# Maxima of two heads in the two row halves of the array, operands loaded in a new row order

## The chip, the cores and the metric

The kernel runs on one core of a Trainium2 chip. The metric is the device time of one execution in microseconds; three runs of the kernel before gave 3184.15, 3186.4 and 3193.72 us.

## What is computed

The reference takes `x` of shape (8, 1024, 256) through four stages, each `x = x + layernorm(stage(layernorm(x)))`: a causal softmax attention with low-rank projections, a feed-forward stage, a causal attention with quadratic features, and a last feed-forward stage with ternary weights. The change touches the two attentions:

```python
# first attention, per batch, 16 heads of width 16
scores = jnp.einsum('bqhd,bkhd->bhqk', Q, K) / math.sqrt(D_K)
scores = jnp.where(causal, scores, -jnp.inf)
attn = jax.nn.softmax(scores, axis=-1)
out = jnp.einsum('bhqk,bkhd->bqhd', attn, V)
...
# second attention: a running sum of features, computed by the kernel as squared scores
num = jnp.einsum('bhtf,bhtfd->bhtd', phi_q, kv_cum)
den = jnp.einsum('bhtf,bhtf->bht', phi_q, jnp.cumsum(phi_k, axis=2))[..., None] + EPS
```

## The kernel before

The program runs nine passes one after the other. Those that matter here: `latent_pass` and `features_pass` compute queries, keys and values of all heads and store them in DRAM; `attend_pass` loads them, once with `softmax=True` (its tiles carry `a_` in the profile) and once with `softmax=False` (`b_`).

**Operands.** Queries and keys are held as three bf16 parts (high, middle, low) whose sum is the f32 value. A product of two such numbers is taken as six products of parts, and these lie under one another as contraction rows: `Q_STACK` and `K_STACK` say which part goes into which group of 16 rows, six groups, 96 rows (`STACK`). In the softmax pass two further rows (96 and 97) hold the negated maximum of each query, split in two, against ones in the keys, so that a score comes out with its maximum already taken off (98 rows).

**Units and rings.** A unit is four heads of one batch with all 1024 positions; there are 32 (`UNITS`). Operands sit in a ring of three buffers (`qs`, `ks`, `vs`). `all_units` runs a loop of ten turns with three units each, and two units behind it.

**SP.** `load(n, r)` issues 13 transfers for a unit: six for the queries, six for the keys, each of 16 rows with 8 KB a row into 16 partitions, and one of 512 KB for the values. The load of unit n+2 is issued when all weighings of unit n-1 are done. `load_rows(n+1)` issues eight small transfers that place the peak rows in `qs`, when VectorE has made them; `store` writes a unit's sums.

**TensorE.** A unit has 12 steps (`STEPS`). Steps 0 to 3 belong to the first half of the queries, with 512, 384, 256 and 128 columns, steps 4 to 11 to the second half, with 512 columns in steps 4 to 8 and 384, 256, 128 in the last three. In step s TensorE computes the scores of step s+2 (`scores`, L896, two heads at a time, two matmuls each) and weighs the values with the exponentials of step s (`weigh`, L910, f32, each head in its own 32 columns of the array). Steps 10 and 11 thus compute the first scores of unit n+1, and `operands` waits there, at step 10, for its load and its peak rows.

**Maxima.** The maximum of each query is found ahead: `maximum_scores` (L886) computes a chunk of up to 512 score columns (queries as the weights of the array) into one of three PSUM banks, VectorE reduces it (`maxima`, L844 a plain maximum, L846 with the causal mask added) and frees the bank. There are 36 chunks per unit, nine per head. Each step has three slots for a chunk: behind the first two scores, behind the second two, and behind the weighing. Slots 0 to 17 of unit n carry the second half of the chunks of unit n+1, slots 18 to 35 the first half of those of unit n+2; at slot 18 TensorE waits for the load of unit n+2 (L930). When the chunks of unit n+1 are done, VectorE closes them (`largest`, L852 to L860) and SP issues the row loads (L735).

**ScalarE and GpSimd.** ScalarE takes the exponentials of two heads at a time from PSUM (L793, squares in the second attention, where VectorE does the fourth head, L820 and L823), GpSimd masks the diagonal blocks (L772).

TensorE and the others take their work strictly in the order in which it is written. The lines that set the places:

```python
                for c in range(a, b):
                    hd, pieces = chunks[c]
                    pe.wait_ge(s_taken, CH * n + c + 1)
...
                    half = CH // 2
                    if k < half and ahead:
                        maximum_scores(n + 1, (r + 1) % RING, half + k, half + k + 1)
                    if k >= half and far:
                        if k == half:
                            pe.wait_ge(loaded[(r + 2) % RING], LOADED * (rnd + (r + 2) // RING) + LOADED)
```

Of the kernel before, what the change touches and what calls it, by code (L numbers as in the profile page):

```python
# [29 lines left out]
F32 = mybir.dt.float32  # L30
# [11 lines left out]
Q_STACK = ((0, 0, 3), (1, 0, 2), (2, 0, 1))  # L42
K_STACK = ((0, 1, 3), (0, 1, 2), (0, 1, 1))
STACK = 16 * 6

# [41 lines left out]
class Resident:  # L87


    def __init__(self, nc, ctx, z):  # L90
# [33 lines left out]
        self.v_dram = nc.dram_tensor("values", [z.UNITS, z.S, P], F32, kind="Internal").ap()  # L124
# [315 lines left out]
def latent_pass(nc, z, m):  # L440
    G, DC, GROUPS = z.G, z.DC, z.TILES // z.G
    with ExitStack() as ctx:
# [18 lines left out]
        def _(sp):  # L461
# [3 lines left out]
            def store(i, u):  # L465
                n = 2 * i + u
                sp.wait_ge(vx_ready, 2 * n + 3)
                for t in range(G):
                    at = u * z.GT + t * P
                    sp.dma_start(m.v_dram[bass.ts(i, z.UPB), at:at + P, :].rearrange("g p k -> p g k"),  # L470
                                 vx[u][:, t, :, :].rearrange("p (g h) k -> p g (h k)", g=z.UPB)).then_inc(stored[u], 16)
# [151 lines left out]
def store_parts(eng, z, m, parts, stored, i, u):  # L623

    for part in range(PARTS):
        for j in range(4):
            eng.dma_start(m.qk_dram[part, j // 2, bass.ds(i * z.D + (j % 2) * P, P), u * z.GT:(u + 1) * z.GT],
                          parts[:, part, j, :]).then_inc(stored, 16)
# [4 lines left out]
def attend_pass(nc, z, m, softmax):  # L633
# [20 lines left out]
    chunks = [(hd, pieces) for hd in range(HPU) for pieces in (  # L654
# [3 lines left out]
    CH = len(chunks)  # L658
    assert CH == 3 * STEPS
    SRING = 3  # L660
    with ExitStack() as ctx:
# [13 lines left out]
        LOADED = 16 * (2 * STACK // z.DK + 1)  # L675
# [4 lines left out]
        if softmax:  # L680
# [8 lines left out]
             rows_ready, ones_ready) = sm("bias_zero", "bias_ready", "peak_set", "s_ready", "s_taken", "npeak_ready",  # L689
                                          "high_ready", "split_ready", "rows_ready", "ones_ready")  # L690
            ROWS_LOADED = 16 * 8
        else:
            twin = sb("twin", [P, 512], F32, 2)
            twin_ready, d_ready = sm("twin_ready", "d_ready")
        block = ctx.enter_context(nc.Block())

# [17 lines left out]
        def _(sp):  # L714
# [1026 lines left out]
```

## Time and profile before

| | us |
|---|---|
| median of three runs | 3186.4 |
| the profiled execution | 3190.47 |
| its span on the core | 3188.3 |
| TensorE busy | 2571.1 (81%) |
| VectorE busy | 2393.3 (75%) |
| ScalarE busy | 1702.3 (53%) |
| GpSimd busy | 918.0 (29%) |
| closing reductions of the softmax pass, first and last start | 301.8 and 1284.6 |
| first score matmul of the second attention | 2282.04 |

A busy share says little by itself: TensorE's work in a matmul pass overlaps, and an average over the span mixes stages. What counts in a stage is the order of events in one unit, which the timeline gives, and who waited for whom. The chain that ended last accounts for the end of the program only (a few per cent of the span), so the two attention passes have to be read from their own stretches.

### The profile page before, as it was taken

The numbers are of one execution on the slowest core, as the hardware profiler recorded it, in microseconds if no ns is written. First come the engines' busy times: TensorE is split into PE (matmuls) and PEld (weight loads), VectorE is DVE, ScalarE is ACT, GpSimd is POOL, SyncE is SP. The second block draws the span as 40 slices with busy tenths as digits, with TensorE's granted clock in tenths as the row PEclk, the third lists the DMA queues.
The fourth block names the chain that finished last, engine by engine and source line by source line (L and its number), as shares of the span: only waits on it lengthen the run. The fifth ranks groups of instructions, "written<-read, shape, count | busy, mean of one in ns | idle before, by whom it ended". The sixth has DMA issues, their size and how long they took to land. (4 is left out here: it accounts for less than half of the span.)

```text
span 3188.3 us, 60438 instructions
## 1 busy us (share of the span) xinstructions
PE 2571.1 (81%) x15239; PEld 1172.0 (37%) x15239; DVE 2393.3 (75%) x5816; ACT 1702.3 (53%) x2778; POOL 918.0 (29%) x844
## 2 busy tenths in 40 slices
PE   2885998988898989576889886878499999995536
PEld 1441332333333333254555554545122222223425
DVE  5886777877787777257999996999476666665975
ACT  0441666655666555443333333766277777773544
POOL 0340111111111111173444442222222222223834
PEclk9895999989999999888999998999699999997879
DMA  5687445454545454240000000455788888863302
GB/s 160 185 270 143 80 74 93 77 89 75 92 79 88 77 90 70 73 165 1 0 0 0 0 0 14 127 163 159 155 141 137 143 135 141 139 119 112 122 10 95
DMA packets 285075, 310.22 MB, mean 97 GB/s; under 512 B 39504, under 2 KB 239136, under 8 KB 272672
## 3 DMA queue, kind: packets, MB, share of 16 engines
q1 hardware_dynamic: 284960, 309.07, 46.4%
q14 instruction: 90, 0.74, 0.1%
q8 instruction: 25, 0.41, 0.1%
HBM read 181.55 MB, written 126.88 MB: 97 GB/s over the span
## 5 line engine op out<-in xcount | busy, mean ns | idle before, releaser
L793 ACT ACTIVATE a_p<-psum 128x1024 f32<-128x1024 f32 (+3 forms) x768 | 590.0, 813 | 385.6 <-PE psum L896 385.3
L846 DVE CUSTOM_DVE_ANT_0 a_dump<-psum,a_bias 128x256 bf16<-128x256 f32 (+3 forms) x1024 | 451.9, 487 | 180.3 <-PE psum L886 154.2
L886 PE MATMUL psum<-a_ks,a_qs 96*128 96x512 bf16 (+3 forms) x1536 | 467.7, 350 | 133.9 <-DMA a_vs<-values 112.7
L793 ACT ACTIVATE b_p<-psum 128x512 f32<-128x512 f32 (+5 forms) x768 | 453.4, 653 | 168.1 <-PE psum L896 167.3
L772 POOL TENSOR_SCALAR_AFFINE_SELECT a_p<-a_p 128x512 f32<-128x512 f32 x256 | 162.9, 636 | 888.5 <-ACT a_p L793 888.5
L896 PE MATMUL psum<-a_qs,a_ks 98*128 98x512 bf16 (+3 forms) x1536 | 395.7, 341 | 5.4 <-ACT a_p L793 3.7
L844 DVE TENSOR_REDUCE a_peak<-psum 128x1 f32<-128x512 f32 x512 | 333.2, 686 | 35.4 <-PE psum L886 34.6
L896 PE MATMUL psum<-b_qs,b_ks 96*128 96x512 bf16 (+3 forms) x1536 | 320.8, 331 | 39.2 <-DMA b_vs<-values 38.9
L910 PE MATMUL psum<-a_p,a_vs 128*32 128x512 f32 (+3 forms) x3072 | 348.3, 527 | 0.6 <-POOL a_p L772 0.4
L820 DVE COPY b_twin<-psum 128x512 f32<-128x512 f32 (+3 forms) x384 | 213.3, 555 | 175.8 <-PE psum L896 174.1
L910 PE MATMUL psum<-b_p,b_vs 128*32 128x512 f32 (+3 forms) x3072 | 328.8, 500 | 8.0 <-POOL b_p L772 8.0
L886 PEld LDWEIGHTS psum<-a_ks,a_qs 96*128 96x128 bf16 x1536 | 135.9, 99 | 497.3 <-issue 163.8
L772 POOL TENSOR_SCALAR_AFFINE_SELECT b_p<-b_p 128x512 f32<-128x512 f32 x256 | 162.8, 636 | 469.6 <-DVE b_p L823 440.2
L1359 PE MATMUL psum<-f_xt,w_fc 128*128 128x512 f32 x512 | 247.8, 646 | 56.6 <-ACT f_xt L1298 50.8
L1121 PE MATMUL psum<-wo,m_att 128*128 128x256 f32 x512 | 146.7, 452 | 125.5 <-POOL m_att L1068 95.9
L823 DVE SCALAR_TENSOR_TENSOR b_p<-psum,b_twin 128x512 f32<-128x512 f32 (+3 forms) x384 | 214.4, 558 | 40.3 <-PE psum L910 0.5
L896 PEld LDWEIGHTS psum<-b_qs,b_ks 96*128 96x128 bf16 x1536 | 109.9, 98 | 343.8 <-issue 174.2
L1269 POOL TENSOR_TENSOR f_parts<-f_rest,f_parts 128x512 bf16<-128x512 f32 x128 | 179.5, 1402 | 167.4 <-DVE f_parts L1228 167.4
L896 PEld LDWEIGHTS psum<-a_qs,a_ks 98*128 98x128 bf16 x1536 | 150.3, 101 | 118.8 <-ACT a_p L793 34.4
L1225 DVE TENSOR_TENSOR f_rest<-f_hid,f_parts 128x512 f32<-128x512 f32 x128 | 191.1, 1493 | 1.6 <-ACT f_parts L1312 1.6
L1370 PE MATMUL psum<-w_proj,f_parts 128*128 128x256 bf16 x1536 | 172.2, 274 | 6.4 <-POOL f_parts L1269 6.4
L1359 PEld LDWEIGHTS psum<-f_xt,w_fc 128*128 128x128 f32 x512 | 105.1, 208 | 191.0 <-issue 183.0
(186 smaller groups left out, 3496.5 us busy)
## 6 DMA issues: line engine op xcount, KB each, us to landing
qk_parts<-l_parts SPq DMA_DIRECT2D x192, 128.0 KB, 1.7
a_qs<-qk_parts SPq DMA_DIRECT2D x192, 128.0 KB, 4.6
a_ks<-qk_parts SPq DMA_DIRECT2D x192, 128.0 KB, 7.6
qk_parts<-g_parts SPq DMA_DIRECT2D x192, 128.0 KB, 1.7
b_qs<-qk_parts SPq DMA_DIRECT2D x192, 128.0 KB, 4.5
b_ks<-qk_parts SPq DMA_DIRECT2D x192, 128.0 KB, 7.6
values<-l_vx SPq DMA_DIRECT2D x64, 256.0 KB, 2.9
a_vs<-values SPq DMA_DIRECT2D x32, 512.0 KB, 10.1
```

The costliest lines, as they stand in the source:

```text
L772: pool.affine_select(out=diag, in_=diag, compare_op=ALU.is_ge, fill=0.0, base=0, pattern=[[0, HPU], [1, P]], channel_multiplier=-1).then_i ...
L793: act.activation(p[s % SLOTS][:, 2 * k:2 * k + heads, q0(s):512], m.psum[:, at:at + heads, q0(s):512], ACT.Exp if softmax else ACT.Square, ...
L820: dve.tensor_copy(twin[s % 2][:, q0(s):512], bank).then_inc(twin_ready, 1)
L823: dve.scalar_tensor_tensor(out=p[s % SLOTS][:, 3, q0(s):512], in0=bank, scalar=1.0 / z.DK, in1=twin[s % 2][:, q0(s):512], op0=ALU.mult, op ...
L844: last = dve.tensor_reduce(dst, piece, AX.X, ALU.max)
L846: last = dve.tensor_tensor_reduce(dump[c % SRING][:, at:at + w], piece, bias[:, 512 - w:], 1.0, NEG, ALU.add, ALU.max, dst)
L886: last = pe.matmul(m.bank[SB + c % SRING][:, at:at + w], qs[r][0:STACK, hd, qt * P:(qt + 1) * P], ks[r][0:STACK, hd, h * 512:h * 512 + w], ...
L896: last = pe.matmul(m.bank[score_bank(s, hd)][:, q0(s):512], ks[r][0:ROWS, hd, kt * P:(kt + 1) * P], qs[r][0:ROWS, hd, h * 512 + q0(s):(h + ...
L910: last = pe.matmul(m.bank[OB[h]][32 * hd:32 * hd + 32, q0(s):512], vs[r][:, kt, 32 * hd:32 * hd + 32], p[s % SLOTS][:, hd, q0(s):512], sta ...
L1225: dve.tensor_tensor(rest[c % 4][:, :], hid[c % 4][:, :], parts[u][:, 0, c, :], ALU.subtract).then_inc(rest_ready, 1)
L1269: pool.tensor_tensor(parts[u][:, 2, j, :], rest[j % 4][:, :], parts[u][:, 1, j, :], ALU.subtract).then_inc(low_ready, 1)
L1359: last = pe.matmul(m.bank[F0 + j % 4], m.w_fc[:, c, j * P:(j + 1) * P], xt[u][:, c, :], start=(c == 0), stop=(c == DC - 1))
```

## The change

The six products of parts get new places, and different ones for heads 0, 1 and heads 2, 3 of a unit. For heads 0 and 1 the four largest products fill rows 0 to 63 and the other two rows 64 to 95. For heads 2 and 3 the three largest fill rows 64 to 111 and the other three rows 0 to 47; rows 48 to 63 are zero. The maxima now use only rows 0 to 63 of a head 0 or 1 and rows 64 to 111 of a head 2 or 3, so the two matmuls of a pair of heads lie in different row halves of the array. A chunk becomes a pair of chunks, 18 per unit, put into the odd slots only; one wait covers both. `EARLY = 6` of the 18 pairs are computed two units ahead, the other 12 one unit ahead, so the last pair of unit n+1 stands in slot 23 of unit n, and the wait for the load of unit n+2 in slot 25.

The peak rows move to rows 112 and 113 (`TOP`). Scores use 114 rows; in the second attention 96 for heads 0 and 1, 112 for heads 2 and 3. Rows that no load fills are filled once per pass by VectorE: 12 fills before its first other work, and TensorE waits for all of them, SP's first load of each buffer for its own.

A load is now 14 transfers of queries and keys with 4 KB a row, ten of them into 32 partitions (two products at a time, their rows interleaved, which is the same in queries and keys) and four into 16, and one for the values, whose DRAM layout changes so that a partition's 4 KB lie together. The order of the parts in DRAM changes to fit (`Q_SLOT`, `K_SLOT`).

```diff
-Q_STACK = ((0, 0, 3), (1, 0, 2), (2, 0, 1))
-K_STACK = ((0, 1, 3), (0, 1, 2), (0, 1, 1))
+Q_SLOT = (1, 2, 0)
+K_SLOT = (1, 0, 2)
 STACK = 16 * 6
+MAIN = 16 * 4
+TOP = 16 * 7
...
-        self.v_dram = nc.dram_tensor("values", [z.UNITS, z.S, P], F32, kind="Internal").ap()
+        self.v_dram = nc.dram_tensor("values", [z.UNITS, P, z.ST, P], F32, kind="Internal").ap()
...
             def load(n, r):
-                for tile, which, stack in ((qs[r], 0, Q_STACK), (ks[r], 1, K_STACK)):
-                    row = 0
-                    for first, step, groups in stack:
-                        for part in range(groups):
-                            src = m.qk_dram[first + step * part, which, bass.ts(n, HPU * z.DK), :]
-                            sp.dma_start(tile[row:row + z.DK, :, :].rearrange("p h t -> p (h t)"),
-                                         src.rearrange("(d h) t -> d (h t)", h=HPU)).then_inc(loaded[r], 16)
-                            row += z.DK
...
+                half = z.S * HPU // 2
+                for par, runs in enumerate((((0, 1, 2, 0, 2), (32, 2, 2, 0, 2), (64, 0, 0, 1, 2)),
+                                            ((64, 1, 2, 0, 2), (96, 2, 1, 1, 1), (0, 2, 1, 0, 1), (16, 0, 0, 1, 2)))):
+                    heads = slice(par * half, (par + 1) * half)
+                    for row, q_slot, q_wide, k_slot, groups in runs:
+                        into = slice(row, row + z.DK * groups)
...
+            for r in range(RING):
+                for tile, fill in ((qs[r], 0.0), (ks[r], 1.0)):
+                    dve.memset(tile[32:MAIN, HPU // 2:HPU, :], 0.0)
+                    last = dve.memset(tile[STACK:P, 0:(HPU if softmax else HPU // 2), :], fill)
+                last.then_inc(rows_set, 1)
...
+                for j in range(a, b):
+                    pe.wait_ge(s_taken, CH * n + 2 * j + 2)
+                    for piece, (qt, h, at, w) in enumerate(chunks[j][1]):
+                        for par in range(2):
+                            hd, half = chunks[j][0] + par * HPU // 2, (slice(0, MAIN), slice(MAIN, TOP))[par]
...
+                    if not softmax or k % 2 == 0:
                         return
...
+                    j = k // 2
+                    if j < CP - EARLY and ahead:
+                        maximum_scores(n + 1, (r + 1) % RING, EARLY + j, EARLY + j + 1)
+                    if j >= CP - EARLY and far:
+                        if j == CP - EARLY:
                             pe.wait_ge(loaded[(r + 2) % RING], LOADED * (rnd + (r + 2) // RING) + LOADED)
```

What stands in a row on TensorE, in the softmax pass, from a weighing in step 4 to the wait for the load in step 6 of a unit (`a_ks1`, `a_qs1`: the buffers of unit n+1; an ISA row is a wait), before:

```order
L910 MATMUL psum<-a_p0,a_vs0 32x512 x4
...
L910 MATMUL psum<-a_p1,a_vs0 32x512 x4
L884 REGISTER_ALU
L886 MATMUL psum<-a_ks1,a_qs1 128x512
L892 REGISTER_ALU
L896 MATMUL psum<-a_qs0,a_ks0 128x512 x2
L930 ISA
L884 ISA
L886 MATMUL psum<-a_ks2,a_qs2 128x128
L886 MATMUL psum<-a_ks2,a_qs2 128x384
```

And now, with a unit in buffer 1, from the weighing of step 6 to the same wait, which stands in step 8:

```order
L937 MATMUL psum<-a_p2,a_vs1 32x512 x4
...
L937 MATMUL psum<-a_p3,a_vs1 32x512 x4
L906 REGISTER_ALU
L910 MATMUL psum<-a_ks2,a_qs2 128x512 x2
L918 REGISTER_ALU
L923 MATMUL psum<-a_qs1,a_ks1 128x256 x2
L918 REGISTER_ALU
L923 MATMUL psum<-a_qs1,a_ks1 128x256 x2
L957 ISA
L906 ISA
L910 MATMUL psum<-a_ks0,a_qs0 128x128 x2
```

The last maxima of the next unit, behind a weighing, and the wait that follows them moved two steps down, toward step 10; each maximum is now two matmuls.

On TensorE in two full steps of the same pass, steps 4 and 5 of a unit, from the first scores of step 5 on, with the new order:

```order
L923 MATMUL psum<-a_qs1,a_ks1 128x512 x2
L906 REGISTER_ALU
L910 MATMUL psum<-a_ks2,a_qs2 128x128 x2
L910 MATMUL psum<-a_ks2,a_qs2 128x384 x2
L918 REGISTER_ALU
L923 MATMUL psum<-a_qs1,a_ks1 128x512 x2
L937 MATMUL psum<-a_p1,a_vs1 32x512 x4
L906 REGISTER_ALU
L910 MATMUL psum<-a_ks2,a_qs2 128x512 x2
```

Before, each of these steps had a maximum behind each of the three groups; now an odd step has a pair in its first and third place and an even step one in its second.

On VectorE at the start of the softmax pass (`a_qs0`, `a_ks0`: buffer 0), before and now:

```order
L830 MEMSET a_ks0 2x4096
L830 MEMSET a_ks1 2x4096
L830 MEMSET a_ks2 2x4096
L832 MEMSET a_peak0 128x64
L846 ISA a_dump0,a_peak0<-psum,a_bias0 128x128
```

```order
L836 MEMSET a_qs0 32x1024
L837 MEMSET a_qs0 32x2048
L836 MEMSET a_ks0 32x1024
L837 MEMSET a_ks0 32x4096
L836 MEMSET a_qs1 32x1024
L837 MEMSET a_qs1 32x2048
```

Three fills became twelve (the rows shown repeat for buffers 1 and 2). In the second attention, where there were none, the same twelve stand with 1024, 1024, 1024 and 2048 elements.

## Rows read from the trace of the kernel before

**Rows 1.** Table of stretches: stretch and length, busy us (count) per engine, clock, DMA.
```profile
core 0: us, PE busy (x) PEld busy (x) DVE busy (x) ACT busy (x) POOL busy (x), PEclk, DMA share, GB/s
500.00:900.00 400.00, 356.45 (x2433) 127.09 (x2433) 311.42 (x1062) 241.55 (x329) 64.80 (x102) 0.94 0.51 84
...
2500.00:2900.00 400.00, 384.59 (x2980) 109.44 (x2978) 273.62 (x497) 307.75 (x537) 104.29 (x164) 0.99 0.77 128
```

**Rows 2.** One line's instructions: the closing reduction of a unit's maxima.
```profile
L852 DVE TENSOR_REDUCE a_npeak<-a_peak x32: 219/220/221, 301.8 to 1284.6; 128x32 f32<-128x64 f32 x32
```

**Rows 3.** TensorE's waits, 330 to 1310 us: total us, times, longest.
```profile
PE psum L886 <- DMA a_vs<-values: 79.8, 26, 4.1
PE psum L886 <- DVE a_peak L846: 17.8, 9, 2.1
```

**Rows 4.** Timeline of TensorE, 664 to 732 us: start, us, instruction.
```profile
667.07 0.60 PE L896 MATMUL psum<-a_qs,a_ks 98*128 98x512 bf16 x2
...
671.25 0.60 PE L896 MATMUL psum<-a_qs,a_ks 98*128 98x512 bf16 x2
...
709.69 0.60 PE L896 MATMUL psum<-a_qs,a_ks 98*128 98x512 bf16 x2
...
710.78 0.38 PE L886 MATMUL psum<-a_ks,a_qs 96*128 96x128 bf16 x2
711.09 1.06 PE L910 MATMUL psum<-a_p,a_vs 128*32 128x512 f32 x8
712.09 0.39 PE L886 MATMUL psum<-a_ks,a_qs 96*128 96x512 bf16 x1
712.31 0.60 PE L896 MATMUL psum<-a_qs,a_ks 98*128 98x512 bf16 x2
...
714.71 0.39 PE L886 MATMUL psum<-a_ks,a_qs 96*128 96x512 bf16 x1
...
719.83 0.39 PE L886 MATMUL psum<-a_ks,a_qs 96*128 96x512 bf16 x1
...
724.02 0.60 PE L896 MATMUL psum<-a_qs,a_ks 98*128 98x512 bf16 x2
...
731.96 0.38 PE L896 MATMUL psum<-a_qs,a_ks 98*128 98x512 bf16 x1
```

**Rows 5.** VectorE's waits, 330 to 1310 us, the one in its own issue.
```profile
DVE a_dump L846 <- issue: 23.4, 10, 2.7
```

**Rows 6.** Timeline of VectorE and of SP's queue, from the closing reduction on.
```profile
716.02 0.22 DVE L852 TENSOR_REDUCE a_npeak<-a_peak 128x32 f32<-128x64 f32 x1
...
717.07 4.96 SPq L735 DMA_DIRECT2D a_qs<-a_rows  x8
```

**Rows 7.** DMA issues: tiles, count, KB each, median us to landing.
```profile
a_qs<-a_rows SPq DMA_DIRECT2D x256, 2.0 KB, 1.8
```

**Rows 8.** Timeline of all engines, 676 to 684 us: a maximum and its reduction.
```profile
676.27 0.39 PE L886 MATMUL psum<-a_ks,a_qs 96*128 96x512 bf16 x1
...
676.85 0.69 DVE L846 CUSTOM_DVE_ANT_0 a_dump<-psum,a_bias 128x512 bf16<-128x512 f32 x1 [0.67 <-PE psum L886]
```

**Rows 9.** Timeline of VectorE in the first unit's maxima, the same chunk two heads apart.
```profile
281.54 0.28 DVE L846 CUSTOM_DVE_ANT_0 a_dump<-psum,a_bias 128x128 bf16<-128x128 f32 x1
...
292.89 0.28 DVE L846 CUSTOM_DVE_ANT_0 a_dump<-psum,a_bias 128x128 bf16<-128x128 f32 x1
```

**Rows 10.** Timeline of all engines at the start of the softmax pass.
```profile
262.76 3.47 DVE L830 MEMSET a_ks<- 2x4096 bf16 x1 [14.62 <-PEq L72]
...
267.03 3.47 DVE L830 MEMSET a_ks<- 2x4096 bf16 x1 [0.80 <-issue]
...
278.05 1.44 PE L886 MATMUL psum<-a_ks,a_qs 96*128 96x128 bf16 x5 [32.87 <-DMA a_vs<-values]
```

**Rows 11.** Timelines of SP's queue and of TensorE at the start of the second attention.
```profile
2265.29 2.67 SPq L724 DMA_DIRECT2D b_qs<-qk_parts  x6
...
2282.04 3.17 PE L896 MATMUL psum<-b_qs,b_ks 96*128 96x512 bf16 x8 [38.90 <-DMA b_vs<-values]
```

More of the change, by code:

```diff
@@ L650, in attend_pass @@
     SLOTS = 4
-    chunks = [(hd, pieces) for hd in range(HPU) for pieces in (
+    chunks = [(hd, pieces) for hd in range(HPU // 2) for pieces in (
         ((0, 0, 0, 128), (2, 0, 128, 384)), ((3, 0, 0, 512),), ((1, 0, 0, 256), (5, 1, 256, 256)),
@@ L657, in attend_pass @@
         ((7, 0, 0, 512),), ((7, 1, 0, 512),))]
-    CH = len(chunks)
+    CP = len(chunks)
+    CH = 2 * CP
     assert CH == 3 * STEPS
     SRING = 3
+    EARLY = 6
     with ExitStack() as ctx:
@@ L674, in attend_pass @@
         st_ready, p_ready, masked, pv_done, o_taken = sm("st_ready", "p_ready", "masked", "pv_done", "o_taken")
[L675 removed]
+        LOADED = 16 * 15
         STORED = 16
@@ L694, in attend_pass, with operand_rows @@
             twin_ready, d_ready = sm("twin_ready", "d_ready")
+        rows_set, = sm("rows_set")
         block = ctx.enter_context(nc.Block())
+        def operand_rows(hd):
+            if softmax:
+                return slice(0, TOP + 2)
+            return slice(0, STACK) if hd < HPU // 2 else slice(0, TOP)
         def q0(s):
@@ L828, in _ @@
                 return
-            for r in range(RING):
-                last = dve.memset(ks[r][STACK:STACK + 2, :, :], 1.0)
-            last.then_inc(ones_ready, 1)
             dve.memset(peak[:, :, :], NEG).then_inc(peak_set, 1)
@@ L837, in maxima @@
             def maxima(n, a, b):
-                for c in range(a, b):
-                    hd, pieces = chunks[c]
+                for c in range(2 * a, 2 * b):
+                    hd, pieces = chunks[c // 2][0] + c % 2 * HPU // 2, chunks[c // 2][1]
                     wait_alone(dve, s_ready, CH * n + c + 1, m.alone)
@@ L877, in _ @@
             pe.sem_inc(pv_done, PV)
-            if softmax:
-                pe.wait_ge(ones_ready, 1)
+            pe.wait_ge(rows_set, RING)
             def maximum_scores(n, r, a, b):
-                for c in range(a, b):
-                    hd, pieces = chunks[c]
-                    pe.wait_ge(s_taken, CH * n + c + 1)
-                    for qt, h, at, w in pieces:
-                        last = pe.matmul(m.bank[SB + c % SRING][:, at:at + w], qs[r][0:STACK, hd, qt * P:(qt + 1) * P],
-                                         ks[r][0:STACK, hd, h * 512:h * 512 + w], start=True, stop=True)
-                    last.then_inc(s_ready, 1)
+                for j in range(a, b):
[3 more added lines that the diff above has]
+                            hd, half = chunks[j][0] + par * HPU // 2, (slice(0, MAIN), slice(MAIN, TOP))[par]
+                            last = pe.matmul(m.bank[SB + (2 * j + par) % SRING][:, at:at + w],
+                                             qs[r][half, hd, qt * P:(qt + 1) * P],
+                                             ks[r][half, hd, h * 512:h * 512 + w], start=True, stop=True)
+                            if piece == len(chunks[j][1]) - 1:
+                                last.then_inc(s_ready, 1)
             def scores(n, r, s, k):
@@ L921, in some_maxima @@
                 def some_maxima(k):
-                    if not softmax:
+                    if not softmax or k % 2 == 0:
                         return
-                    half = CH // 2
-                    if k < half and ahead:
-                        maximum_scores(n + 1, (r + 1) % RING, half + k, half + k + 1)
-                    if k >= half and far:
-                        if k == half:
+                    j = k // 2
[3 more added lines that the diff above has]
+                        if j == CP - EARLY:
                             pe.wait_ge(loaded[(r + 2) % RING], LOADED * (rnd + (r + 2) // RING) + LOADED)
-                        maximum_scores(n + 2, (r + 2) % RING, k - half, k - half + 1)
+                        maximum_scores(n + 2, (r + 2) % RING, j - CP + EARLY, j - CP + EARLY + 1)
                 for s in range(STEPS):
```

47 lines of the change are left out of this document (30 added, 17 removed).

## Prediction, made before the changed kernel ran

> **What bounds the kernel now.** I read the table of stretches first [rows 1]. In the softmax attention pass TensorE is busy 356.45 of 400 us at a granted clock of 0.94, VectorE 311.42, ScalarE 241.55; in the second attention pass TensorE has 384.59 of 400 us at 0.99. So both passes are TensorE's, and only the first has time between its instructions. The first pass is a chain of 32 units: the reduction that closes a unit's maxima starts 32 times between 301.8 and 1284.6 us [rows 2], 982.8 / 31 = **31.70 us per unit**.
>
> What fills a unit is read from TensorE's timeline where the clock is high and nothing waits [rows 4]: steps 4 to 11, 0 and 1 run from 709.69 to 731.96 (22.27 us), steps 2 and 3 from 667.07 to 671.25 (4.18 us), together 26.45 us. The waits [rows 3] are 79.8 / 31 = 2.57 us per unit for the loads of the unit after next (met at slot 18 of 36) and 17.8 / 31 = 0.57 us for VectorE. The last follows stalls of up to 2.7 us in VectorE's own issue, ten of them, one per turn of the loop [rows 5]. 31.70 - 26.45 - 3.14 leaves 2.1 us, the price of the stretches at the lower clock: 6% off the mean clock of a 31.7 us unit is 1.9.
>
> **The gain: maxima in pairs.** A full step [rows 4] takes 2.62 us (709.69 to 712.31) and has three maxima of 512 columns at 0.22 (712.09 to 712.31). Run two heads at a time, 18432 columns of a unit become 9216: at 0.22 per 512 that takes 18 x 0.22 = 4.0 us off a unit. No row here shows two row halves at work together; the nearest is the weighing, whose eight f32 pieces in four column strips take 1.00 us (711.09 to 712.09). I take full overlap, and keep none at all for a rival.
>
> **The gain: the load.** The wait of 2.57 us goes, whatever the new transfers take: slot 18 becomes slot 25, two steps (over 4 us) later, and the longest wait was 4.1 us [rows 3]. Transfers that land sooner are then worth nothing more.
>
> **What takes the place of that wait.** Before, the maxima of unit n+1 end at slot 17 of unit n; with EARLY = 6 they end at slot 23, and the scores of unit n+1 still begin at step 10. Between lies a chain: last maximum, VectorE, four small VectorE operations, eight loads of peak rows from SP, TensorE. Before [rows 4, 6, 7]: slot 17 at 714.71, the closing reduction at 716.02, the first row load at 717.07, eight issues of 4.96 us to 722.03, and the last, issued about 0.6 us before that, lands 1.8 us after its issue, at 723.2. Step 10 starts at 724.02, so 0.8 us was to spare.
>
> After, from the start T of the pair in slot 23: 0.58 us to VectorE (676.27 to 676.85 [rows 4, 8]), two reductions of 0.63 and 0.69, a gap of 0.1, so the closing reduction starts at T+2.0; then 1.05 + 4.96 + 1.2 as before: rows there at **T+9.2**. TensorE gets to step 10 sooner. VectorE finishes the pair at T+1.9, the small operations at T+3.0, the first chunk of the pair of slot 25 at T+3.7, of slot 27 at T+5.0; the pair of slot 29 needs that, and step 10 is reached at T+5.3. TensorE then stands still 3.9 us in each unit, SP, VectorE and ScalarE behind it. The load that SP issues for the next unit isn't moved by it.
>
> **The rest of the cycle**, from step 10 to the pair of slot 23 of the next unit, is ten steps with 15 pairs. Before it took 22.26 us [rows 4]: 724.02 to 731.96, plus 4.18, plus 709.69 to 719.83. VectorE takes 18 chunks from 281.54 to 292.89 [rows 9], 0.63 each, 1.26 per pair. But a pair may only start when one chunk is left to VectorE (three banks), and from the end of a reduction to the start of the next, through TensorE, 0.67 us pass [rows 8]; with 0.63 of cover and the start of a waiting instruction I take 1.35 per pair, 1.26 at least. In two full steps TensorE has twice a pair, a weighing and one head pair's scores (0.22 + 1.09 + 0.43 = 1.74), and once a pair and both scores (0.22 + 0.87 = 1.09, VectorE's 1.35 counts): 4.83, so the four full steps 9.7 against 10.1 before. The six narrow steps have nine pairs, VectorE's: 12.1, what they take now. Together 21.8 us; with 1.26 throughout 9.5 + 11.3 = 20.8.
>
> A warm unit is then 9.2 + 21.8 = 31.0 us. VectorE's issue stall stays, 0.6. The wait of 3.9 us is as long as the one that goes, so the clock falls after it as now; half of the work behind it is VectorE's, which doesn't feel the clock, so I take 1.4 instead of 2.1. **33.0 us per unit, 1.3 more than now, 31 x 1.3 = +40 us.** The low end is 9.2 + 20.8 with 0.3 for all else, 30.3 (-43 us).
>
> **Switching between shapes.** A weighing starts 0.31 us after the maximum ahead of it (710.78 to 711.09), where one of the same shape follows after 0.22, and its 1.00 us (to 712.09) is 0.12 over the 0.88 of four streams of 512 columns at 0.22. Entering and leaving another shape thus shows 0.21 us, beside full-array instructions. A pair between scores enters and leaves too. My sum puts this at nothing, since part of the 0.21 may be the f32 weight loads'; with it in full, a pair holds TensorE 0.43: two full steps 1.95 + 1.95 + 1.35 = 5.25, the four 10.5, the narrow ones 12.7 where TensorE and VectorE hold each other up, a unit 9.2 + 23.2 + 0.6 + 1.8 = 34.8.
> The Trainium skill, page "TensorEngine Tiling (Array Packing)", section "Key Properties", says that a change of tiling mode drains the engine, while tiles of one mode run in parallel; by its first half the unit is the 34.8 us just given, by its "Theoretical Speedup" alone 33.0. The 0.31 against 0.22 speaks for a drain; nothing in this trace shows one for row halves.
>
> **Starts of the two passes.** The new fills count, by the program, 8192 elements per buffer in the first pass (zeros are filled two to an element). Fills of 4096 start 4.27 us apart (262.76 to 267.03 [rows 10]): three buffers 25.6 us, to 288.4, and TensorE waits for all; it began at 278.05: **+10** (+6 by their 3.47 us of busy time). The first load waits 8.5 us for its buffer's fills and then takes its 16 us at most, to 288, so no more. The first unit's maxima are VectorE's in both versions and the shorter second set there only uncovers the row chain: 0, within 3 either way. In the second pass 5120 elements per buffer are 16.0 us, against the 16.75 us that TensorE waits anyway (2265.29 to 2282.04 [rows 11]); the load starts 5.3 us later and may be faster: 0 to +5, taken as **+2**. Its steady part stays, since TensorE is full and 112 rows stream like 96. The stores of values keep their number and size, with rows that lie further apart: 0 (up to +5).
>
> **Sum**: 40 + 10 + 2 = +52 us. The profiled execution took 3190.47 us with a span of 3188.3 and lies 4.1 us above the median of 3186.4; I set the sum on the median: **3238 us**. A measurement of this kernel tells about 0.3%, 10 us, from no change.
>
> **Rivals.**
> *Faster (0.20)*: the pass is freed as meant. VectorE isn't held up between pairs and the clock, with TensorE less loaded but never far behind, hardly falls: 30.3 us per unit, -43 + 12 = -31, 3155 us. For it: VectorE needs only 36 x 0.63 + 1.05 = 23.7 us per unit, ScalarE 19. Against: the row chain of 9.2 us starts a third of a unit later than now. It decides at 31.0 us per unit, below that the kernel is faster.
> *The drain (0.22)*: 34.8 us per unit, +96 + 12 = +108, 3294 us. For it the 0.31 against 0.22, against it that no row shows the halves.
> *The halves don't overlap (0.05)*: a pair costs 0.44 and the switches 0.21: two full steps 2.17 + 2.17 + 1.52, the four 11.7, the narrow ones 12.1 + 9 x 0.21 = 14.0, 37.3 per unit, +174 + 12 = +186, 3372 us. The change then doesn't do what it says.
> *No change (0.10)*: the two effects cancel at 31.3 us per unit, 3186 us with the longer start.
> *The forecast (0.43)*: 32 to 34 us per unit, 3207 to 3270 us, taken at 33.0.
>
> **Range and chances.** From 3160, which leaves out the better half of the faster case, to 3320, which leaves out the serial case and the worst of the drain. Slower by over 0.3%: 0.43 + 0.22 + 0.05 = 0.70; within: 0.10; faster: 0.20.
>
> **What would show it.** The closing reductions of the first pass stand 33 us apart; the waits of TensorE show one for the peak rows about 31 times, near 4 us, and none for the values; the loads land well ahead; matmuls of the two halves start together or 0.22 us apart, and the first score matmul behind a pair comes after 0.22 or more like 0.43; VectorE's waits for maxima shorten but don't vanish; TensorE begins the first pass near 288 us and the second near 2280 to 2287, shifted by what came before. I am wrong if the rows are there before step 10, which needs the chain in under 5.5 us, or if the four full steps between end up far under 9.5 us.

## The result, and the profile after

The changed kernel took **3293.8 us** (median of four runs, 3290.6 to 3297.7), the kernel before, run beside it, 3190.1 us: a ratio of 1.0315, with an interval of 1.0295 to 1.0335. It is slower by 103.8 us. Forecast were +52 us, 3238, with a range of 3160 to 3320.

From the page of the changed kernel, the two groups of TensorE's matmuls in the softmax pass, scores (L923) and maxima (L910), with busy us, mean ns, and the idle time ahead of them:

```profile
L923 PE MATMUL psum<-a_qs,a_ks 114*128 114x512 bf16 (+3 forms) x1536 | 394.0, 363 | 122.6 <-DMA a_qs<-a_rows 119.3
...
L910 PE MATMUL psum<-a_ks,a_qs 64*128 64x512 bf16 (+7 forms) x1536 | 243.0, 356 | 146.0 <-DVE a_peak L870 64.6
```

The table of stretches, with the columns of [rows 1], in the softmax pass and in the second attention:

```profile
500.00:900.00 400.00, 327.39 (x2268) 83.43 (x2266) 296.70 (x980) 229.53 (x308) 59.22 (x94) 0.90 0.27 80
...
2600.00:3000.00 400.00, 383.75 (x2972) 109.36 (x2968) 272.49 (x496) 306.83 (x536) 104.02 (x164) 0.99 0.43 128
```

The second attention is what it was, TensorE full, with half the DMA share. In the softmax pass every engine does less per microsecond than before: TensorE 327 of 400 us where it had 356, VectorE 297 where it had 311 [rows 1]. Nothing became the bound by being full. The closing reductions, which answer to [rows 2], tell the length of a unit:

```profile
L876 DVE TENSOR_REDUCE a_npeak<-a_peak x32: 219/220/222, 318.0 to 1378.4; 128x32 f32<-128x64 f32 x32
```

1060.4 / 31 = **34.2 us per unit** against 31.70. That alone is 77.6 us. The whole of the span's +104.3 us (3292.6 against 3188.3) divides at these two reductions and at the first score matmul of the second attention (2381.88 now, 2282.04 before [rows 11]):

| stretch | before | after | difference |
|---|---|---|---|
| start to the first closing reduction | 301.8 | 318.0 | +16.2 |
| 31 units | 982.8 | 1060.4 | +77.6 |
| last closing reduction to the second attention's first score | 997.4 | 1003.5 | +6.1 |
| from there to the end | 906.3 | 910.7 | +4.4 |

TensorE's waits in the softmax pass, 350 to 1380 us (total, times, longest), beside [rows 3]:

```profile
PE psum L923 <- DMA a_qs<-a_rows: 112.8, 30, 3.9
PE psum L910 <- DVE a_peak L870: 50.0, 71, 1.2
PE psum L910 <- DVE a_peak L868: 26.1, 38, 2.1
```

The wait for the values is gone. In its place is one for the peak rows, in every unit, 112.8 / 30 = 3.76 us each. The chain behind it, from the timeline of all engines (start, us, instruction; SPq is the issue of SP's queue), from the pair in slot 23 to the scores of step 10:

```profile
728.58 0.39 PE L910 MATMUL psum<-a_ks,a_qs 64*128 64x512 bf16 x2
...
730.50 0.22 DVE L876 TENSOR_REDUCE a_npeak<-a_peak 128x32 f32<-128x64 f32 x1
...
731.86 5.00 SPq L757 DMA_DIRECT2D a_qs<-a_rows  x8
...
738.13 1.89 PE L923 MATMUL psum<-a_qs,a_ks 114*128 114x512 bf16 x4 [3.70 <-DMA a_qs<-a_rows]
```

From 728.58 to 738.13 are 9.55 us. The last row shows a second thing: four score matmuls take 1.89 us there, and 1.05 where TensorE has been busy for a while (718.99 below). The granted clock is 0.50 from 738.2 to 740.0 us, which is half speed, the 1.2 GHz level, and it comes right behind the wait.

Finally the pairs, from TensorE's timeline: a row that bounds the full steps, then a pair between scores, a pair behind a weighing and one ahead of a weighing:

```profile
718.99 1.05 PE L923 MATMUL psum<-a_qs,a_ks 114*128 114x512 bf16 x4
...
721.40 0.60 PE L923 MATMUL psum<-a_qs,a_ks 114*128 114x512 bf16 x2
721.93 0.39 PE L910 MATMUL psum<-a_ks,a_qs 64*128 64x128 bf16 x4
722.26 0.60 PE L923 MATMUL psum<-a_qs,a_ks 114*128 114x512 bf16 x2
...
723.79 0.39 PE L910 MATMUL psum<-a_ks,a_qs 64*128 64x512 bf16 x2
724.11 1.04 PE L923 MATMUL psum<-a_qs,a_ks 114*128 114x512 bf16 x4
725.08 0.39 PE L910 MATMUL psum<-a_ks,a_qs 64*128 64x512 bf16 x2
725.40 1.06 PE L937 MATMUL psum<-a_p,a_vs 128*32 128x512 f32 x8
```

Two matmuls of 512 columns together last 0.39 us, as one did before (714.71 in [rows 4]): the two halves do work at the same time. But the next instruction comes 0.32 us after the pair (725.08 to 725.40), and the pair itself starts late: four score matmuls at 0.22 would end 0.86 us after 724.11, the pair starts after 0.97. Between scores, 0.86 us pass from the two score matmuls at 721.40 to those at 722.26; the scores alone take 0.43 of it, so the pair holds TensorE 0.43 us, and two single maxima held it 0.44.

### The profile page after: what moved, and what is told of

It is laid out like the page before. It is cut to its first block and busy times, and to the rows that moved or that the text cites. A ratio compares the mean times of both kernels' runs of the same rounds, so it can differ in the third digit from the quotient of the medians.

```text
span 3292.6 us, 60468 instructions
## 1 busy us (share of the span) xinstructions
PE 2543.1 (77%) x15239; PEld 1082.0 (33%) x15239; DVE 2436.9 (74%) x5837; ACT 1706.1 (52%) x2778; POOL 917.0 (28%) x844
## 5 line engine op out<-in xcount | busy, mean ns | idle before, releaser
L870 DVE CUSTOM_DVE_ANT_0 a_dump<-psum,a_bias 128x128 bf16<-128x128 f32 (+3 forms) x1024 | 445.2, 488 | 75.9 <-PE psum L910 70.0
L923 PE MATMUL psum<-a_qs,a_ks 114*128 114x512 bf16 (+3 forms) x1536 | 394.0, 363 | 122.6 <-DMA a_qs<-a_rows 119.3
L910 PE MATMUL psum<-a_ks,a_qs 64*128 64x512 bf16 (+7 forms) x1536 | 243.0, 356 | 146.0 <-DVE a_peak L870 64.6
L923 PE MATMUL psum<-b_qs,b_ks 96*128 96x512 bf16 (+7 forms) x1536 | 320.9, 330 | 41.4 <-DMA b_vs<-values 40.8
L1386 PE MATMUL psum<-f_xt,w_fc 128*128 128x512 f32 x512 | 250.1, 651 | 58.1 <-ACT f_xt L1325 52.2
L923 PEld LDWEIGHTS psum<-a_qs,a_ks 114*128 114x128 bf16 x1536 | 105.0, 101 | 413.2 <-issue 211.8
L923 PEld LDWEIGHTS psum<-b_qs,b_ks 96*128 96x128 bf16 (+1 forms) x1536 | 110.2, 98 | 345.0 <-issue 214.6
L910 PEld LDWEIGHTS psum<-a_ks,a_qs 64*128 64x128 bf16 (+1 forms) x1536 | 59.8, 95 | 414.1 <-DVE a_peak L870 190.9
L1148 PEld LDWEIGHTS psum<-wo,m_att 128*128 128x128 f32 x512 | 116.9, 234 | 163.2 <-issue 108.6
```

Source lines behind the costliest of these rows:

```text
L870: last = dve.tensor_tensor_reduce(dump[c % SRING][:, at:at + w], piece, bias[:, 512 - w:], 1.0, NEG, ALU.add, ALU.max, dst)
L910: last = pe.matmul(m.bank[SB + (2 * j + par) % SRING][:, at:at + w], qs[r][half, hd, qt * P:(qt + 1) * P], ks[r][half, hd, h * 512:h * 512 ...
L923: last = pe.matmul(m.bank[score_bank(s, hd)][:, q0(s):512], ks[r][live, hd, kt * P:(kt + 1) * P], qs[r][live, hd, h * 512 + q0(s):(h + 1) ...
L1148: last = pe.matmul(bank, att[u][:, c, t * P:(t + 1) * P], wo[:, c, :], start=(c == 0), stop=(c == DC - 1))
L1386: last = pe.matmul(m.bank[F0 + j % 4], m.w_fc[:, c, j * P:(j + 1) * P], xt[u][:, c, :], start=(c == 0), stop=(c == DC - 1))
```

## The experiments

Each kernel was measured against the kernel before on the same chip (its median was 3192.8 us in the first set, 3196.0 in the second). "A" is my theory throughout: the place of the last maxima, ahead of a chain of 9 us, sets the unit, and the clock behind the wait adds to it.

### Nine pairs early in place of six

The changed kernel with one number changed, so that the last pair of unit n+1 stands in slot 17, where its last chunk stood before.

```diff
-    EARLY = 6
+    EARLY = 9
```

> The changed kernel with EARLY = 9: nine pairs two units ahead and nine one unit ahead, so that the last pair of the next unit stands in slot 17 again, as before the change, and the wait for the load in slot 19. Theory A (the chain from the last maximum to the peak rows sets the unit, 34.2 us): TensorE's wait of 3.8 us for the peak rows is gone and with it most of the lower clock; the closing reductions stand about 29.5 us apart, the kernel takes some 3150 us. Theory B (the switches between array shapes and the round trip between TensorE and VectorE cost it, the wait only fills time that would be lost anyway): the reductions stay 33 us apart or more, 3255 us or more. The loads, now in 12 us after the unit's start, are there at slot 19 in both.

Measured: **3125.0 us**, ratio 0.9797 (0.9772 to 0.9822). A unit takes (1210.7 - 317.5) / 31 = 28.8 us. The closing reduction, TensorE's waits from 350 to 1180 us, and that stretch in the table (clock 0.99, third value from the end):

```profile
L876 DVE TENSOR_REDUCE a_npeak<-a_peak x32: 219/220/222, 317.5 to 1210.7; 128x32 f32<-128x64 f32 x32
```
```profile
PE psum L910 <- DVE a_peak L870: 58.1, 90, 2.5
...
PE psum L910 <- DMA a_vs<-values: 15.3, 15, 1.6
```
```profile
350.00:1180.00 830.00, 747.17 (x5564) 201.35 (x5560) 718.02 (x2436) 554.53 (x754) 147.52 (x232) 0.99 0.30 92
```

The wait for the rows is gone and the clock is back with it, as theory A had it; the unit came out shorter than its 29.5 us. Of the change, the 12 pairs that stood one unit ahead instead of nine cost 169 us: 5.4 us per unit. Over this stretch TensorE's idle time per unit is 3.6 us less than in the changed kernel (82.8 us in 28.8 units against 157.8 in 24.3), and its busy time, for the same matmuls, 1.8 us less (25.9 against 27.7 us per unit), which goes with the clock (0.99 against 0.90). One place shows the clock's part by itself, steps 10 and 11 of a unit, at full clock here and behind the wait in the changed kernel:

```profile
706.61 1.04 PE L923 MATMUL psum<-a_qs,a_ks 114*128 114x512 bf16 x4
...
710.51 0.61 PE L923 MATMUL psum<-a_qs,a_ks 114*128 114x256 bf16 x4
```

They take 3.90 us, against 6.07 for the same instructions there (704.67 to 710.74, shown further below).

### The late place alone, in the kernel before

The kernel before with 24 chunks one unit ahead and 12 two units ahead, in place of 18 and 18: the same shift, without pairs, new loads or fills.

```diff
-                    half = CH // 2
-                    if k < half and ahead:
-                        maximum_scores(n + 1, (r + 1) % RING, half + k, half + k + 1)
+                    early = CH // 3
+                    late = CH - early
+                    if k < late and ahead:
+                        maximum_scores(n + 1, (r + 1) % RING, early + k, early + k + 1)
```

> The kernel before with the place of the maxima alone changed: 24 of the 36 single chunks one unit ahead, 12 two units ahead, so that the last chunk of the next unit stands in slot 23 and the wait for the load in slot 24. Theory A: the wait for the loads (2.57 us a unit) goes and one for the peak rows of about 4.4 us comes (the chain of 8.5 us against 4.2 us for steps 8 and 9); the unit goes from 31.7 to 33.5 or 34, the kernel to about 3250 us. Theory B (only pairs make the place harmful): the unit falls to 28 or 29 us, the kernel to about 3090 us.

Measured: **3299.3 us**, ratio 1.033 (1.0306 to 1.0355), 35.0 us per unit. The closing reduction and the wait for the rows, 350 to 1180 us:

```profile
L852 DVE TENSOR_REDUCE a_npeak<-a_peak x32: 219/220/223, 301.6 to 1387.7; 128x32 f32<-128x64 f32 x32
```
```profile
PE psum L896 <- DMA a_qs<-a_rows: 74.4, 23, 3.6
```

The place alone makes the kernel before as slow as the whole change does: +3.3 us per unit. The wait it makes is 3.2 us per unit (74.4 / 23), and the wait for the values that it takes away was 2.57 [rows 3]; the granted clock of 350 to 1180 us fell from 0.93 to 0.88. The difference of the two waits, 0.6, is the small part of it. TensorE's idle time in that stretch went from 3.4 to 4.6 us per unit (its waits for VectorE grew too, from 0.7 to 1.35), and its busy time, for the same matmuls, from 28.3 to 30.4: 2.1 of the 3.3 us go with the clock. The expectation for theory A was a wait of 4.4 us and a unit of 33.5 to 34; the wait came out shorter and the unit longer.

### The pairs without the row halves

The changed kernel with both matmuls of a pair over rows 0 to 111, so that they can't overlap.

```diff
-                            hd, half = chunks[j][0] + par * HPU // 2, (slice(0, MAIN), slice(MAIN, TOP))[par]
+                            hd, half = chunks[j][0] + par * HPU // 2, slice(0, TOP)
```

> The changed kernel with its pairs as they are, but each maximum taken over rows 0 to 111 (all six products) instead of one row half, so the two matmuls of a pair follow each other in the full array, without a change of shape and without overlap. The trace of the changed kernel shows a pair of 512 columns at 0.32 us plus 0.11 ahead of it, 0.43 together. Theory A (the change of shape costs what the overlap saves): a pair takes 0.44, the unit stays within 0.3 us of 34.2 and the kernel within 10 us of 3294. Rival (the overlap brings its 4 us a unit and the switches are free): the unit grows by 2 us or more where TensorE is the bound, the kernel by 60 us or more.

Measured: **3316.8 us**, ratio 1.0374 (1.0345 to 1.0403), (1405.9 - 319.0) / 31 = 35.06 us per unit: 0.86 more than the changed kernel, 23 us in all. The granted clock of 350 to 1180 us is 0.94 here and 0.90 there, and the wait for the rows 3.5 us instead of 3.76, so the 0.86 is what remains after both. From its timeline:

```profile
732.33 0.61 PE L910 MATMUL psum<-a_ks,a_qs 112*128 112x512 bf16 x2
732.86 1.07 PE L937 MATMUL psum<-a_p,a_vs 128*32 128x512 f32 x8
733.86 0.60 PE L923 MATMUL psum<-a_qs,a_ks 114*128 114x512 bf16 x2
734.30 0.60 PE L910 MATMUL psum<-a_ks,a_qs 112*128 112x128 bf16 x4
734.74 0.60 PE L923 MATMUL psum<-a_qs,a_ks 114*128 114x512 bf16 x2
...
736.27 0.61 PE L910 MATMUL psum<-a_ks,a_qs 112*128 112x512 bf16 x2
736.71 1.03 PE L923 MATMUL psum<-a_qs,a_ks 114*128 114x512 bf16 x4
```

Two matmuls here last 0.61 against 0.39, so the halves do overlap in the changed kernel. A pair over all rows holds TensorE 0.44 us between scores (734.30 to 734.74), in the halves 0.43: no gain. Ahead of a weighing it is 0.53 (732.33 to 732.86) against 0.43 with the entry, behind one 0.44 (736.27 to 736.71) against 0.32 (723.79 to 724.11). So the overlap is worth 0.1 us where the neighbour on one side is a weighing, which changes shape anyway, and nothing elsewhere; 12 of a unit's 18 pairs have such a neighbour. Neither number expected of this run came out: it lies between the 10 us of A and the 60 of its rival.

### The loads alone

The kernel before with the new loads and nothing else: single maxima in the old places, 98 rows, no fills of zeros. Since each transfer carries all four heads it has 8 KB a row, 256 KB, and a unit takes seven transfers (13 before, 15 in the changed kernel). The values have the changed layout.

```diff
-Q_STACK = ((0, 0, 3), (1, 0, 2), (2, 0, 1))
-K_STACK = ((0, 1, 3), (0, 1, 2), (0, 1, 1))
+Q_SLOT = (1, 2, 0)
+K_SLOT = (1, 0, 2)
...
+                for row, q_slot, q_wide, k_slot in ((0, 1, 2, 0), (32, 2, 2, 0), (64, 0, 0, 1)):
+                    into = slice(row, row + 2 * z.DK)
+                    src = parts[0][:, q_slot:q_slot + (1 if q_wide else 2), :]
+                    if q_wide:
+                        src = src.to_broadcast([z.DK, 2, z.S * HPU])
+                    sp.dma_start(q[into, :], src).then_inc(loaded[r], 16)
+                    sp.dma_start(k[into, :], parts[1][:, k_slot:k_slot + 2, :]).then_inc(loaded[r], 16)
+                sp.dma_start(vs[r][:, :, :], m.v_dram[bass.ts(n, 1), :, :, :].rearrange("n p k c -> p (n k) c")
```

> The kernel before with the loads alone changed: two products at a time into 32 partitions with their rows interleaved (six transfers of 256 KB for queries and keys), the values laid out so that a partition's 4 KB lie together; 96 and 98 rows, single maxima and their slots as before, no new fills. Theory A: the load lands before slot 18, TensorE's wait of 2.57 us a unit goes with part of the lower clock (2.1 us), nothing else moves in; 28 us a unit, 31 x 3.5 = 110 us less, about 3080 us. Rival (the load is not what the wait is for, or the peak rows, with 0.8 us to spare, take its place): a unit of 30.5 us or more, 3150 us or more.

Measured: **3049.0 us**, ratio 0.9548 (0.9527 to 0.957): the fastest of all, 27.4 us per unit. The closing reduction, the only wait of TensorE above 2.1 us in all from 350 to 1180 us, that stretch, and the load of the values with its landing (median us):

```profile
L854 DVE TENSOR_REDUCE a_npeak<-a_peak x32: 219/220/220, 297.4 to 1148.0; 128x32 f32<-128x64 f32 x32
```
```profile
PE psum L888 <- DVE a_peak L848: 17.9, 9, 2.1
```
```profile
350.00:1180.00 830.00, 805.54 (x5813) 289.89 (x5809) 714.72 (x2458) 581.78 (x795) 155.11 (x244) 1.00 0.36 93
```
```profile
a_vs<-values SPq DMA_DIRECT2D x32, 512.0 KB, 6.5
```

TensorE is busy 806 of 830 us at full clock. A unit is 4.26 us shorter than before; the wait for the values, 2.57, and the price of the lower clock, which the prediction had put at 2.1, come to 4.7. The nine-pair version above, whose loads differ from these in rows of 4 KB and 15 transfers, is 76 us slower: 1.4 us per unit, and 20 us more ahead of the first closing reduction (317.5 against 297.4). Per unit its TensorE waits 2.0 us for VectorE (58.1 / 28.8), here 0.6, and 0.5 for the values, here nothing; that last part may be the loads' and not the pairs', and without it 0.9 us per unit remain. **The pairs, with their row order and its fills, are a loss even in the right place.**

### The row loads from two queues

The changed kernel, with four of a unit's eight row loads issued from ScalarE, behind its exponentials of step 11, and four from SP. This shortens the chain and touches nothing else.

```diff
-                for k in range(2):
-                    at = qs[r][TOP + k:TOP + k + 1, :, :].rearrange("o h (q b i) -> o (h q) b i", b=4, i=32)
...
+                place_rows(sp, n, r, 0)
...
+                    if s == STEPS - AHEAD - 1 and softmax and ahead:
+                        place_rows(act, n + 1, (r + 1) % RING, 1)
```

> The changed kernel, its order of pairs unchanged (last pair of the next unit in slot 23), with four of the eight loads of peak rows issued by ScalarE instead of SP. This shortens the chain to the peak rows by the issue of four transfers, 4 x 0.62 = 2.5 us, and leaves all else. Theory A (that chain sets the unit): TensorE's wait for the rows falls from 3.8 to about 1.4 us, the unit from 34.2 to 31.7 or, with part of the lower clock given back, to 30.5; the kernel takes 3190 to 3215 us. Theory B (the wait is slack that something else would fill, or what counts is when the transfers land and not their issue): less than 1 us of the unit goes, 3265 us or more.

Measured: **3265.6 us**, ratio 1.0232 (1.02 to 1.0265); a unit takes (1354.4 - 317.6) / 31 = 33.45 us, 0.75 less than in the changed kernel. The wait for the rows, 350 to 1180 us, and the issues in the timeline:

```profile
PE psum L929 <- DMA a_qs<-a_rows: 72.0, 25, 3.2
```
```profile
721.12 2.46 SPq L728 DMA_DIRECT2D a_qs<-a_rows  x4
...
722.68 2.49 ACTq L728 DMA_DIRECT2D a_qs<-a_rows  x4
...
726.44 1.89 PE L929 MATMUL psum<-a_qs,a_ks 114*128 114x512 bf16 x4 [2.76 <-DMA a_qs<-a_rows]
```

The expectation had the chain 2.5 us shorter. ScalarE was still at its exponentials when the rows were ready and issued 1.56 us behind SP, so the chain ended 5.0 - (1.56 + 2.49) = 0.95 us sooner. The wait fell by 0.88 us (3.76 to 72.0 / 25 = 2.88) and the unit by 0.75: microsecond for microsecond, nearly. The chain sets the unit. By its numbers alone, 0.75 us and 3265.6 us, the run falls to the rival (under 1 us, 3265 or more), because the shortening was smaller than planned; what speaks for A is that the unit gave back nearly all of it.

### Single maxima in one row half

The kernel with the loads alone, with its maxima over rows 0 to 63 in place of 0 to 95. They leave out two of the six products, the smallest; everything else is computed in full.

```diff
-                        last = pe.matmul(m.bank[SB + c % SRING][:, at:at + w], qs[r][0:STACK, hd, qt * P:(qt + 1) * P],
-                                          ks[r][0:STACK, hd, h * 512:h * 512 + w], start=True, stop=True)
+                        last = pe.matmul(m.bank[SB + c % SRING][:, at:at + w], qs[r][0:64, hd, qt * P:(qt + 1) * P],
+                                          ks[r][0:64, hd, h * 512:h * 512 + w], start=True, stop=True)
```

> The kernel with the loads alone changed (27.4 us a unit), where each maximum, still one by one in the old slots, is taken over rows 0 to 63 only, which hold the four largest products. No two of them can overlap, so this measures what a change between the full array and a row half costs. If it is what the changed kernel's timeline shows (0.11 us ahead of a maximum and 0.10 behind it, of which one is there already next to a weighing), a step grows by 0.42 us, a unit by 5 us where TensorE is the bound, to about 32 us, the kernel to about 3200 us. If the change of shape is free and only the f32 weighing costs something, the unit and the time stay as they are, 3049 us.

Measured: **3222.0 us**, ratio 1.008 (1.0052 to 1.0109), (1314.3 - 298.9) / 31 = 32.75 us per unit, 5.3 more than with 96 rows. From TensorE's timeline:

```profile
707.17 0.39 PE L898 MATMUL psum<-a_qs,a_ks 98*128 98x256 bf16 x2
707.49 0.39 PE L888 MATMUL psum<-a_ks,a_qs 64*128 64x128 bf16 x2
707.82 0.39 PE L898 MATMUL psum<-a_qs,a_ks 98*128 98x256 bf16 x2
708.14 0.39 PE L888 MATMUL psum<-a_ks,a_qs 64*128 64x512 bf16 x1
708.46 1.06 PE L912 MATMUL psum<-a_p,a_vs 128*32 128x512 f32 x8
```

512 columns hold TensorE 0.32 us at every step here, where they hold it 0.22 among full-array matmuls: 0.11 into the half, 0.10 out of it. The same columns on fewer rows cost more. Of the 36 maxima 12 stand between scores and pay both, 0.21; 12 stand ahead of a weighing and 12 behind one, and pay one of the two, since the other switch is there anyway. That is 12 x 0.42 = 5.0 of the 5.3 us, as expected before the run. This is the cleanest sight of the price that the prediction's sum left out.

### Six units per turn of the loop

The kernel with the loads alone, whose only wait left follows VectorE's issue stalls at the turn of the loop, with turns half as many and twice as long (and the fills of ones on GpSimd).

```diff
-            with eng.Fori(0, ROUNDS) as i:
-                for r in range(RING):
-                    unit(RING * i + r, r, i, True, True)
+            turns = 2 if softmax else 1
+            with eng.Fori(0, ROUNDS // turns) as i:
+                for q in range(turns * RING):
+                    unit(turns * RING * i + q, q % RING, turns * i + q // RING, True, True)
```

> The kernel with the loads alone changed (3049 us), with two further edits: the loop of the softmax pass takes six units a turn instead of three (five turns), and the three fills of ones are done by GpSimd behind its own mask, so that VectorE and TensorE start the pass without them. If VectorE's issue stalls (9 or 10 of 2 to 2.7 us, one per turn) belong to the turn of the loop, five of them go with the lower clock behind each, 15 us or so; the start gains another 4 us: about 3030 us. If they come with the number of instructions fetched, they stay: 3045 us.

Measured: 3051.5 us, ratio 0.9559 (0.9533 to 0.9586), which is the time without the edit; 27.46 us per unit. VectorE's stalls are gone from the list of waits, and in their place TensorE has its own:

```profile
PE psum L898 <- issue: 14.2, 4, 4.1
```

The 15 us expected of the stalls' end didn't come: four pauses of TensorE of up to 4.1 us took the place of nine waits of up to 2.1. The 4 us expected at the start didn't come either; TensorE began the pass at 274.09 us, waiting for the values, and at 273.67 with the loads alone, and the first closing reduction stands at 297.8 against 297.4. Nothing was won, and I took it no further.

## Why the prediction came out as it did

**The chain of the peak rows**: right, and the cause of the loss. Forecast T+9.2 us, measured 9.55, 0.3 of the difference in VectorE's small operations (730.50 to 731.86, 1.36 us where 1.05 was taken); a wait of 3.9 us about 31 times, measured 3.76 and 30. The late place alone, the early pairs and the two queues show it from three sides.

**The wait for the load goes, and faster transfers are worth nothing more**: right for this kernel. Queries and keys land in a median of 2.9 and 3.0 us, values in 4.4, and no wait for them is left. But the step hid what was worth most: with the maxima left where they were, the loads alone gain 144 us. The Trainium skill, page "SBUF — State Buffer", section "Door 1: The DMA port swizzle", says that a transfer's bandwidth depends on how many of the SBUF's ports its partitions reach, and by its map 32 neighbouring ones reach twice those of 16. The changed kernel agrees in direction, with transfers of one row length side by side: 128 KB into 32 partitions land in hardly more time than 64 KB into 16.

```profile
a_qs<-qk_parts SPq DMA_DIRECT2D x160, 128.0 KB, 2.9
...
a_qs<-qk_parts SPq DMA_DIRECT2D x64, 64.0 KB, 2.8
```

How much of the 144 us is due to this, to the fewer transfers or to the values' longer rows, no run parts.

**A unit at 33.0 us**: this is the step that failed, by 1.2 us, 37 of the 52 us by which the sum is short, and the term that was mis-sized most is the clock's. I had taken 1.4 instead of 2.1, on the ground that "half of the work behind it is VectorE's, which doesn't feel the clock". In the trace the matmuls behind the wait are scores and weighings that VectorE doesn't cover:

```profile
704.67 1.89 PE L923 MATMUL psum<-a_qs,a_ks 114*128 114x512 bf16 x4 [3.89 <-DMA a_qs<-a_rows]
...
710.74 0.61 PE L923 MATMUL psum<-a_qs,a_ks 114*128 114x256 bf16 x4
```

Before, from 724.02 [rows 4] to this row:

```profile
727.99 0.38 PE L896 MATMUL psum<-a_qs,a_ks 98*128 98x256 bf16 x2
```

Steps 10 and 11 took 6.07 us here and 3.97 before, so these two alone lost 2.1, 0.7 more than the 1.4 allowed for the whole unit; with nine pairs early the same instructions took 3.90 at full clock. The other terms of this unit, which has no stall of VectorE's, are small: steps 0 to 3 8.25 us (710.74 to 718.99) where 8.15 was taken, the four full steps up to the pair of slot 23 9.59 (718.99 to 728.58) where 9.7 was, the chain 0.35 over. Together that is 33.46 us, and the stalls, in every third unit, bring the mean to 34.2, 0.75 where 0.6 was taken. The granted clock fell, as this stretch of both kernels shows, before and then after:

```profile
350.00:1180.00 830.00, 740.81 (x4983) 261.51 (x4982) 640.81 (x2181) 498.79 (x675) 131.91 (x208) 0.93 0.51 83
```
```profile
350.00:1180.00 830.00, 672.23 (x4658) 171.79 (x4656) 614.12 (x2042) 466.79 (x631) 124.35 (x196) 0.90 0.26 77
```

**Switching between shapes**: "My sum puts this at nothing" was wrong; the drain rival had the size exactly, 0.43 us for a pair between scores. The error is not in the 1.2 us above, though: the sum had let VectorE's pace of 1.35 us set one pair in three, and the full steps came out as forecast. The rival's 5.25 us for two full steps were a little too long (5.12, 718.99 to 724.11), since only one of their three pairs stands between scores; next to a weighing, which switches anyway, the pair pays half. The Trainium skill, page "TensorEngine Tiling (Array Packing)", section "Key Properties", says that tiles of one mode run in parallel and that a change of mode drains the engine. Both fit what the trace shows, 0.39 us for the two matmuls of a pair and 0.21 us more around it. This price, 0.21 us for in and out, equals what the overlap of 512 columns saves (0.22). Of the gain of 4.0 us per unit, the six pairs between scores thus brought nothing and the 12 beside a weighing 0.1 each, 1.2 us, where TensorE is the bound. The drain rival's total, 3294 us, is the measured one by luck: its unit of 34.8 us is 0.6 too long, 19 us in all, and outside the units it had 12 us where 26.7 were measured.

**The start of the pass**: TensorE began at 289.35 us, forecast 288.4. But "the first unit's maxima are VectorE's in both versions", taken as 0 within 3, failed. They ran from 289.35 to 318.0, 28.65 us, where they had taken 23.75:

```profile
289.35 0.61 PE L910 MATMUL psum<-a_ks,a_qs 64*128 64x128 bf16 x4 [43.56 <-DVE a_ks L837]
...
297.39 0.61 PE L910 MATMUL psum<-a_ks,a_qs 64*128 64x512 bf16 x2 [1.02 <-DVE a_peak L870]
...
298.89 0.61 PE L910 MATMUL psum<-a_ks,a_qs 64*128 64x512 bf16 x2 [0.89 <-DVE a_peak L868]
299.65 1.29 DVE L868 TENSOR_REDUCE a_peak<-psum 128x1 f32<-128x512 f32 x2 [0.21 <-PE psum L910]
```

These pairs come every 1.5 us, forecast 1.26 to 1.35. The granted clock is 0.50 from 289.35 to 318 us, but it was 0.50 from 278 to 301.8 before too, so the lower clock alone isn't the reason. Nor is either engine full: TensorE is busy 11.4 and VectorE 24.5 of the 28.65 us, while single maxima had kept VectorE busy 22.8 of 23.8. A pair needs two of the three banks, so TensorE starts it when VectorE has one chunk left, and at this clock that chunk is done 0.21 us before the pair's first maximum is there. The same happens with the pairs over full rows (first closing reduction at 319.0), and not with single maxima in a row half (298.9, against 297.4 with 96 rows). Of the start's +16.2 us, 11.3 are the fills and 4.9 this.

**The second attention**: its fills begin at 2363.39 and its scores at 2381.88, 18.5 us against 16.75 [rows 11], +1.7 where +2 was forecast. The other 4.3 us between the last closing reduction and these fills, where only the stores of values stood (0, up to +5), and the 4.4 behind are not placed by any run. For the first, the spread is as large: the changed kernel took 1003.5 us, and with full rows and with two queues, where the code of this stretch is the same, 1008.4 and 995.0. For the second, the kernels with new loads took 907 to 911 us and the two with the old ones 906, so a few us may be the loads'.

**Direction and range** held. The 0.70 for slower was well placed; but the forecast and the drain weren't alternatives: both mechanisms were there at once, the drain with half its price.

## What to carry to other kernels

Before moving work later, count the chain that hangs on its last piece, transfers and their issue included, to the instruction that needs it, and give a new wait twice: once as itself, once as half-speed work behind it. Tiles in row halves paid here only beside instructions that switch anyway; alternating with full-array matmuls of 512 columns, two for the price of one costs two. What a long run of one shape would bring, no run here shows at full clock. Where a change has several parts, the one that no sum values (here the loads, 4.5% faster by themselves) is worth a run of its own.

## What was unexpected of the hardware

- A matmul of 512 columns on 64 rows between full-array ones holds TensorE 0.32 to 0.33 us, on 96 rows 0.22: fewer rows, 5.3 us more per unit.
- The granted clock of 350 to 1180 us was 0.90 where TensorE waited 3.8 us once per unit, and 0.99 and 1.00 in the nine-pair kernel and the one with the loads alone, which have no such wait. TensorE was idle for 83 of 830 us in the first of these all the same, in shorter pieces.
- Loads of the same bytes took half the DMA engines' time: share 0.51 at 83 GB/s before, 0.26 at 77 GB/s after, 0.36 at 93 GB/s with the loads alone. How much of it is the 32 partitions, and how much the 4 KB rows of the values, no run parts.
- A longer loop body moved the issue stalls from VectorE (2.3 us, up to 2.7 [rows 5]) to TensorE, 14.2 us in four pieces, instead of removing them.
